# Matmuls without a use in TensorE's waits, weights loaded in the first microseconds: cross attention and two-expert feed-forward, 16 batches

## The reference, cut to what matters

```
x = x + gamma * attention(layernorm(x), ctx, ctx)      # 16 batches of 128 x 256, 8 heads of 16 rows
                                                      # softmax over 256, along the free axis of x
n = layernorm(x)
expert = argmax(softmax(n @ Wg.T))                    # 2 experts
out0 = gelu(n @ W0a.T + b0a) @ W0b.T + b0b            # 256 -> 512 -> 256
out1 = relu(n @ W1a.T + b1a) @ W1b.T + b1b
x = x + (out0 where expert == 0, else out1)
```

## Time and profile before

| | |
|---|---|
| time, median of 3 runs | 248.19 us (248.04 to 249.8) |
| the profiled execution: its own time | 248.95 us |
| its span, first to last instruction | 247.1 us |
| busy: PE, DVE, ACT, POOL | 219.7, 178.1, 144.6, 96.3 us |
| chain that ended last: PE, DVE, ACT, issue | 72%, 12%, 9%, 5% |
| mean granted clock of PE | 0.979 |

### The profile page before, as it was taken

One profiled execution on the slowest core, in us unless ns is written; L12 is line 12 of the kernel. 1 busy time (PEld: TensorE's weight loads), 2 busy tenths in 40 slices (PEclk: granted clock), 3 DMA queues, 4 the chain that ended last, 5 costly groups with the idle time before them and its releaser, 6 DMA issues.

```text
span 247.1 us, 5173 instructions
## 1 busy us (share of the span) xinstructions
PE 219.7 (89%) x2001; PEld 171.3 (69%) x2001; DVE 178.1 (72%) x368; ACT 144.6 (59%) x217; POOL 96.3 (39%) x128
## 2 busy tenths in 40 slices
PE   0477988777898999999999999999999989979995
PEld 0344544444577888788878887888788877959995
DVE  7667476999875988698869886987597715445573
ACT  2012454856667758775877587758774786644140
POOL 8440231333984822482248224823361054032000
PEclk9999999886799999999999999999999999999999
DMA  4227777723330525161516250514111000000101
GB/s 170 100 71 246 247 298 224 273 90 129 88 131 36 183 66 175 10 233 64 176 25 216 65 175 21 178 49 150 20 49 53 16 24 3 21 21 3 41 5 42
DMA packets 18954, 25.86 MB, mean 105 GB/s; under 512 B 1946, under 2 KB 12530, under 8 KB 18674
## 3 DMA queue, kind: packets, MB, share of 16 engines
q1 hardware_dynamic: 17782, 22.63, 27.8%
q10 hardware_dynamic: 1148, 2.90, 3.3%
HBM read 11.28 MB, written 2.10 MB: 54 GB/s over the span
## 4 chain that ended last, share of the span: by engine, by line
PE 72%; DVE 12%; ACT 9%; issue 5%; POOL 0%; DVEq 0%; ACTq 0%; POOLq 0%
PE ff L822 18%; PE ff L852 11%; PE od L765 8%; PE st L753 8%; PE ff L863 6%; PE smax L741 5%; DVE nmax L396 4%; ACT P L600 4%; PE st L728 3%; PE od L773 3%; ACT hid L637 2%; PE od L780 2%; PE smax L714 2%; PE tr L795 1%; DVE qkst L184 1%
## 5 line engine op out<-in xcount | busy, mean ns | idle before, releaser
L600 ACT ACTIVATE P<-st 128x1024 f32<-128x1024 f32 x64 | 65.6, 1025 | 54.1 <-PE st L753 45.6
L396 DVE TENSOR_REDUCE nmax<-smax 128x4 f32<-128x1024 f32 x54 | 66.1, 1224 | 28.8 <-PE smax L741 28.2
L262 POOL TENSOR_TENSOR mv<-mv,power 128x1 f32<-128x1 f32 x31 | 18.3, 591 | 69.2 <-DVE mv L361 69.2
L280 POOL TENSOR_TENSOR hidL<-hid,hidH 128x1024 fp32r<-128x1024 f32 x13 | 31.0, 2387 | 20.6 <-DVE hidH L456 16.2
L822 PE MATMUL ff<-xnTh,w1h 128*128 128x256 f32 x128 | 37.5, 293 | 1.0 <-DVE y L494 1.0
L753 PE MATMUL st<-qkst 64*128 64x256 f32 x240 | 31.1, 338 | 6.6 <-ACT P L600 6.5
L637 ACT ACTIVATE hid<-ff,b1t 128x256 f32<-128x256 f32 x64 | 26.7, 470 | 17.4 <-PE ff L822 17.3
L822 PE MATMUL ff<-xnTh,w1l 128*128 128x256 f32 x128 | 36.0, 281 | 0.0
L822 PE MATMUL ff<-xnTl,w1h 128*128 128x256 f32 x128 | 35.9, 281 | 0.0
L765 PE MATMUL od<-P,vt 128*32 128x256 f32 x512 | 35.7, 426 | 0.1
L852 PE MATMUL ff<-w2h,hidH 128*128 128x256 f32 x124 | 34.2, 309 | 0.0
(11 more groups left out here) (100 smaller groups left out, 344.8 us busy)
## 6 DMA issues: line engine op xcount, KB each, us to landing
qkst<-parts SPq DMA_DIRECT2D x45, 256.0 KB
xv<-in_xv SPq DMA_DIRECT2D x16, 256.0 KB, 2.8
qk<-in_qk SPq DMA_DIRECT2D x15, 256.0 KB, 3.6
out<-y SPq DMA_DIRECT2D x16, 128.0 KB, 2.5
w1t<-in_w ACTq DMA_DIRECT2D x1, 1024.0 KB, 5.4
w2t<-in_w ACTq DMA_DIRECT2D x1, 1024.0 KB, 4.7
qk<-in_first SPq DMA_DIRECT2D x1, 256.0 KB, 3.8
qk<-in_first ACTq DMA_DIRECT2D x1, 256.0 KB, 3.9
```

What stands on the lines that cost most here:

```text
L262: pool.tensor_tensor(mv[:, b % 2, 11:12], mv[:, b % 2, 10:11], power[:, 0:1], ALU.pow).then_inc(s_rstd, 1)
L280: pool.tensor_tensor(hidL[:, units, :], hid[:, units, :], hidH[:, units, :], ALU.subtract).then_inc(s_hidL, 1)
L396: dve.tensor_reduce(nmax[:, c % 2, :, :, j].rearrange("p a e -> p e a"), (ff if c in WIDE and j % 2 else smax)[:, :, :, :], AX.X, ALU.max, ...
L600: act.activation(P[:, b % 2, j, :, :, :].rearrange("p e a l -> p (e a l)"), st[:, :, :, :].rearrange("p e a l -> p (e a l)"), ACT.Exp, sca ...
```

## The change

- **Matmuls without a use.** A new helper `spin` issues matmuls of `onesb` (ones) with `hid` (zeros there, read as 512 bf16 columns) into `od` or `tr`, whose contents nobody needs at that time: 14 before the first real matmul, and 3 to 7 in the slots of the table `SPIN`, 65 in all, the last in slot 15. Each stands in PE's list behind the slot's `maxima`.
- **Weights.** ACT issues `w1t`'s load behind its first two rows instead of in slot 2, and `w2t`'s behind the first `high` instead of in slot 6; the four small loads move from slot 0 to slot -2. The splits move from batches 2 and 3 to batches 1 and 2 on ACT, and from batch 3 to batch 2 on POOL. `gate_and_bias` moves from slots 6 to 12 to slots 0 to 6.
- **Batch 2** is prepared in slot -4, behind the last `take_max0`, instead of in slot -7.
- **One of the four places of `qkst`** is filled by ACT (two ACTIVATEs) instead of DVE (two MEMSETs). DVE sets `onesb` and `hid` first.

```diff
-EARLY = {2: -7, 3: -2}
+EARLY = {2: -4, 3: -2}
+SPIN_FIRST = 14
+SPIN = {-6: 3, -5: 3, -4: 5, -2: 7, -1: 4, 0: 4, 1: 4, 2: 4, 3: 4, 4: 3, 6: 3, 7: 3, 8: 3, 10: 3, 11: 3, 12: 3, 14: 3, 15: 3}
...
+            def spin(bank, count):
+
+                for _ in range(count):
+                    pe.matmul(bank, onesb[:, :], hid[:, 0, :].bitcast(BF16), start=True, stop=True)
...
+                if n <= PAIRS:
+
+                    spin(od[:, :], SPIN.get(n, 0))
+                elif j == 0 and b < 4:
+                    pe.wait_ge(s_mrow, b)
+                    spin_transposes(b)
...
-            fill(dve, 1)
+            dve.memset(onesb[:, :], 1.0).then_inc(s_ones, 1)
+            dve.memset(hid[:, 0, :], 0.0).then_inc(s_ones, 1)
...
-                if 6 <= n < 13:
-                    gate_and_bias(n - 6)
+                if 0 <= n < 7:
+                    gate_and_bias(n)
...
+            act.wait_ge(s_const, 1)
+            for side in range(2):
+
+                act.activation(qkst[:, 1, :, side, :], power[:, 0:1].unsqueeze(2).to_broadcast([128, PAIRS, L]), ACT.Copy,
+                               scale=-2.0 * side).then_inc(s_fill[1], 1)
+            act.dma_start(w1t[:, :, :, :].rearrange("p a e f -> p (a e f)"), w1).then_inc(s_w1, 16)
...
+            act.dma_start(w2t[:, :, :].rearrange("p u l -> p (u l)"), w2).then_inc(s_w2, 16)
```

More of the change, by code:

```diff
@@ L339, in _ @@
                     masks(b - 2)
-                if b == 3 and j >= 2:
+                if b == 2 and j >= 2:
                     pool.wait_ge(s_w2h, j - 1)
@@ L343, in _ @@
                     pool.tensor_tensor(w2l[:, half, :], w2t[:, half, :], w2h[:, half, :], ALU.subtract).then_inc(s_w2l, 1)
-                if b == 3 and j < LC:
+                if b == 2 and j < LC:
                     pool.wait_ge(s_w1h, j + 1)
@@ L662, in _ @@
                     copy_max0()
[L663 to L672, removed]
+                if b == 1 and j < LC:
                     act.wait_ge(s_w1, 16)
                     act.activation(w1h[:, j, :, :], w1t[:, j, :, :], ACT.Copy).then_inc(s_w1h, 1)
-                if b == 3 and j < 2:
+                if b == 2 and j < 2:
                     act.wait_ge(s_w2, 16)
@@ L680, in _ @@
                     high(p)
+                if n == -2:
+                    act.dma_start(wgb[:, :, :].rearrange("p a c -> p (a c)"), wg.partition_broadcast(128)).then_inc(s_small, 16)
+                    act.dma_start(gam[:, :], gamma.partition_broadcast(128)).then_inc(s_small, 16)
+                    act.dma_start(bias_f[:, :], b2.partition_broadcast(128)).then_inc(s_small, 16)
+                    act.dma_start(b1t[:, :], b1).then_inc(s_small, 16)
                 if k == 0 and 2 <= c <= B:
@@ L704, in _, with spin_transposes @@
         def _(pe):
+            def spin(bank, count):
+                for _ in range(count):
+                    pe.matmul(bank, onesb[:, :], hid[:, 0, :].bitcast(BF16), start=True, stop=True)
+            def spin_transposes(b):
+                if b >= 3:
+                    pe.wait_ge(s_xTl, b - 2)
+                spin(tr[:, :, :, :], SPIN.get(n, 0))
             def maxima0(j):
@@ L830, in begin @@
                     pe.wait_ge(s_w2, 16)
-                    pe.wait_ge(s_bias, 7)
-                    pe.wait_ge(s_ones, 2)
+                    pe.wait_ge(s_bias, 8)
                 pe.wait_ge(s_hid, UNITS * (b // 2) + (UNITS if t else UNITS - 2))
@@ L868, in low_pass @@
                     mm.then_inc(s_lastg, 1)
+            pe.wait_ge(s_ones, 2)
+            spin(od[:, :], SPIN_FIRST)
             for n in range(-LEAD, SLOTS):
@@ L909, in _ @@
                         low_pass(b - 4, 0)
+                    if 1 <= b < 4:
+                        pe.wait_ge(s_mrow, b + 1)
+                        spin_transposes(b)
                     if b >= 2:
@@ L912, in _ @@
                 if j == 3 and b >= 1:
+                    if b < 4:
+                        pe.wait_ge(s_ods, b)
+                        spin(od[:, :], SPIN.get(n, 0))
                     transpose_od(b - 1)
```

6 lines of the change are left out of this document (2 added, 4 removed).

## The result

| | before | predicted | changed kernel |
|---|---|---|---|
| median, us | 248.56 (same chip, beside it) | 243.3 (240.9 to 246.6) | 252.97 (251.04, 252.2, 253.74, 254.81) |
| ratio to before | | 0.979 | 1.013, 95% interval 1.008 to 1.019 |
| profiled execution: own time / span | 248.95 / 247.1 | 244.05 | 254.81 / 253.0 |
| first layer's first matmul | 68.42 | 63.5 | 74.35 |
| from there to the end of the span | 178.7 | 178.7 | 178.65 |

The prediction was wrong in sign.

A forecast was written before the change was run, and what follows sets the result against it. PE bounds from 76 us on; before that, PE at the low clock with DVE close behind. 2.8 - 1.4 + 0.2 + 2.0 = 3.6, + 1.4, less 0.1: 4.9 us off 248.95, 244.05; median 243.3 (240.9 to 246.6).

The forecast's parts named there:

- w1t costs nothing: it is issued at 4.8 and moves in 6 to 9.5 us: At the start: w1's early load is free, as it moves while the DMA engines stood still before.
- PE would now be about nine tenths busy: Slots -1 to 2: argument that PE, two thirds busy when its clock fell before, would now stay at the high clock.
- rival C: Clock stays low, decided in slots -1 to 2: added matmuls cost 0.43 us each, +10 to +12, 259 us; chance 0.07.
- 2.1 us of its issue time: ACT ahead of the first exponential: the four small loads take 25.19 to 27.28 in the trace before; exponential predicted at 20.4.
- the first layer starts 37.9 us after that reduction: Slots 1 to 16: from batch 2's first reduction to the first layer 37.9 us instead of 39.3.
- the 1.4 us that were to arrive of PE's 5: Slots 1 to 16: three faster `values` save PE 5 us, of which only 1.4 reach the first layer; DVE 89% busy.
- The stall of 0.8 us behind POOL's splits: Batch 2: `rstd` of batch 1 comes at 57.9 behind the splits, where DVE wants it at 57.1.
- the splits ran beside DVE before too: POOL's splits moved into batch 2: rows of DVE lengthened beside them, but the sum the same with or without the move.
- The reductions without `moments1` between them: Start: batch 2's `moments1` leaves batch 0's reductions; these start at 9.0 to 12.75, the last 2.8 us earlier.
- the slot of 2.4 us: First four slots: 3.1 us for the first, then 2.4 each, instead of 3.2 before.
- my later bound: Batch 1's stacks, loaded beside w2: landing at 15.8 us if w2 goes ahead, 14.8 at even shares; 16.0 taken for `maxima(1)`.
- Rival D: Slot 0: late small loads hold up `gate_and_bias(0)` and DVE's list, each us late one lost; at 28, 246.3; chance 0.10.

The follow-up runs named there:

- e5: e1 with the four small loads and gate_and_bias also back in slots 0 and 6 to 12; 249.3 us, ratio 1.002.
- e12: e9 with w2's load also moved to slot 3, behind the small loads; 244.4 us, ratio 0.978.
- e1: Changed kernel with w1's load issued behind ACT's first K conversion, which waits for batch 1's q and k; 250.27 us, ratio 0.996.
- e4: Kernel before with w1's load alone moved up, right behind ACT's first load; 250.22 us, ratio 1.004.
- e6: Changed kernel with the four small loads and gate_and_bias back in slots 0 and 6 to 12; 253.19 us, ratio 1.019.
- e11: Changed kernel with POOL's four splits alone back in batch 3; 253.45 us.
- e3: Kernel before with only the added matmuls, their waits and the two fills that they read; 250.61 us, ratio 1.002.
- e8: e5 with POOL's four splits back in batch 3; 246.96 us, ratio 0.990.
- e9: e8 with the small loads issued in slot 3 instead of slot 0; 245.43 us, ratio 0.985.
- e7: Kernel before with a list of useless matmuls of three forms ahead of PE's first real one, to test the clock; 290.0 us, compared with nothing.
- e10: e9 without any of the added matmuls; 248.71 us, ratio 0.997.

## Why the prediction was wrong, step by step

Where its steps start, in us of the trace (e5 has w1 and the small loads mended, e12 the whole mended version):

| | predicted | changed | e5 | e12 |
|---|---|---|---|---|
| first `maxima0` | 7.8 | 9.73 | 7.92 | 7.98 |
| last reduction of batch 0 | 12.75 | 18.75 | 13.46 | 13.52 |
| `transpose_max` | 14.1 | 20.74 | 15.45 | 14.89 |
| `maxima(1)` | 16.0 | 21.30 | 17.24 | 15.20 |
| first exponential | 20.4 | 27.27 | 20.70 | 18.76 |
| first reduction of batch 2 | 25.5 | 34.65 | 26.06 | 24.12 |
| slot 4's scores (before: 32.80) | | 43.61 | 32.78 | 30.83 |
| first layer | 63.5 | 74.35 | 69.18 | 64.33 |

**"w1t costs nothing: it is issued at 4.8 and moves in 6 to 9.5 us" is the step that failed first.** I took an ACT-issued DMA to stand in line behind the ACTIVATEs ahead of it. The trace has it at 1.54 us, ahead of them. A wait ahead of it in the list does hold it (in e1 it is issued at 5.64, when q and k are there, and not after the conversion of 0.42 us), but the nearest wait here was for a fill that starts at 0.72 us. So 1 MB ran beside batch 1's q and k; 2.6 us later data (8.22 against 5.64 in e1) and 1.7 us later first maxima (9.73 against 8.07). e1 shows the effect in the changed kernel (2.7 us), e4 the same load's price alone (1.3 us).

**That the added groups hold the clock, for "PE would now be about nine tenths busy", failed next**, and is rival C for slots -6 to 3. Two things were wrong in it. The 14 first matmuls end at 6.67, as predicted ahead of 7.7, but then PE stands for 3.07 us, and the first real matmul runs at clock 0.57. In the three kernels with this hole (the changed one, e6, e11; gaps of 2.7 to 3.4 us) the clock fell in the hole or within 0.2 us of its end; in e1, e3, e5, e8, e9 and e12, where the gap was 0.9 to 2.0 us, it was high there and the rows of the first `maxima0` took 0.48 us or less, not 0.64 to 0.80. And once low it stayed so until about 22.8 us, though PE was busy for all of it, since this stretch is mostly `maxima0`'s form, with 3 to 5 added ones between; e7 shows that this form alone does not hold the clock. It fell in that stretch without the hole too, only later: in e3 and e8 at about 11 us, in e1, e5 and e9 at about 13; in e12 alone it did not. e3 is the plainest case: no hole, and still low for 10 us. With the clock low each added matmul is on the path: at 0.43 us, as rival C had priced it (3 + 3 + 5 of them stand ahead of `transpose_max`). Of the 6.0 us from 12.75 to 18.75, 1.9 are the late data. From the first `maxima0` to the last reduction it is 9.0 us, against 5.5 in e5, so 3.5 go with the low clock, and 0.6 my walk had missed anyway. That the hole brings the clock down at once rests on the comparison of these nine traces; no run changed the hole alone.

**The small loads: "2.1 us of its issue time"** were 3.5 us (23.73 to 27.22), of which one took 2.16, in the same microseconds in which SP issued the three copies of the stacks for 3.47 us. In e1 it was another of the four, 2.28 us, again beside such copies (3.23 us); in e5, issued at 23.18, each took 0.33 to 0.48 us. Why one issue waits is open; I saw it only beside SP's, and not each time: `b1t` in e5, at 24.53 beside copies issued from 24.44 on, took 0.45. Its price in the changed kernel is the exponential at 27.27, 3.06 us behind the start of the scores instead of 2.0, a new hole of PE of 1.59 us, and another fall of the clock, from about 30 until about 43, which e1 shows too behind its hole of 2.43 us and e5 and e6, without one, don't (in e5 it falls at about 33, behind the wait for `mlow`). That is the way from 6.9 us behind the forecast at the exponential to 9.2 at the first reduction of batch 2, and to slot 4 at 43.61. By the rows, moving the small loads back is worth 6.7 us at slot 4 in the changed kernel (e6) and 8.0 in e1 (e5), both single executions. The times show 1.0 us in e5 and nothing in e6, since `gate_and_bias` moved back with them: its copies met the split, and its work came to lie where DVE is the bound. The first of these e8 shows; the second is argued, from DVE's 30.05 us of work behind slot 4 in e9 against 27.9 in the changed kernel. No run moved the loads alone.

**Slots 1 to 16: "the first layer starts 37.9 us after that reduction"** failed last: the 1.4 us that were to arrive of PE's 5 did not. `values` did get fast (1.93 us three times, 4.7 us less in all). But from the first reduction of batch 2 to the first layer it took 39.7 us in the changed kernel, 43.1 in e5 and 40.2 in e12 (39.3 before). In the changed kernel the loss lies ahead of slot 4: 9.0 us to there, at the low clock, where it was 3.7 before; from slot 4 on it took 30.7 us against 35.6. Some of that is DVE's: four of the seven steps of `gate_and_bias` were done by then, and DVE is busy 27.9 us there and not 31.1. In the mended kernels it is the other way round: DVE is the bound, as predicted, at 90% in e9 (33.3 us from slot 4), and PE's gain ends in waits of its own, of which the one for `mlow` at slot 4 is 1.7 us in e5 and in e12. The stall of 0.8 us behind POOL's splits was 0.23 (DVE for the `rstd` ahead of `x_norm` at 69.22). The splits do hold the rows of DVE that they stand beside. The timeline of the changed kernel:

```profile
58.29 0.98 DVE L438 TENSOR_SCALAR xn<-x,mv 128x256 f32<-128x256 f32 x1
...
59.63 2.35 POOL L349 TENSOR_TENSOR w1l<-w1t,w1h 128x1024 fp32r<-128x1024 f32 x1
...
60.79 1.35 DVE L388 TENSOR_SCALAR qk<-qk,mv 128x256 f32<-128x256 f32 x1
```

`q_norm` takes 1.35 us there and 0.40 elsewhere. The forecast had seen this for `x_norm` and put it at no change, as "the splits ran beside DVE before too". For the changed kernel that was nearly right: before, the pair took 0.99 and 0.73 a batch later, and e11 shows no gain from moving the splits. It fails where they meet other rows: in e5 the same splits made 3.27 us of three copies that take 0.91, and e8 against e5, the splits moved alone, is 2.3 us. The Trainium skill's SBUF — State Buffer (SBUF: two separate sides) names the cause, a pair of ports that DVE and POOL lock from each other; the rows agree, and a move of such work changes which rows it meets.

**What was right.** The reductions without `moments1` between them, the slot of 2.4 us (2.46 in e5), `values` at the high clock, and 178.7 us for the rest. `values` was fast all three times only in the changed kernel, e1 and e11, though: e5, e8, e9 and e12 each have one or two slow ones (2.37 to 3.41 us). w2 beside batch 1's stacks was right in kind: 1.15 us of waiting in e5, where the forecast had 1.4, but `maxima(1)` 1.2 us later (16.0 taken, itself 0.2 beyond my later bound; 17.24 in e5; 15.20 without w2). With the first load out of the way e5 was 0.3 us from the forecast at the first exponential and 0.6 at batch 2's first reduction. Some of that is luck: the 1.2 us of `maxima(1)` were made up by the 0.9 that the forecast had given to the small loads ahead of the exponential, which e5 does not have there. Rival D was half right: a transfer did take PE's place (in e5 and e12), not `gate_and_bias`'s inputs, but those of slot 4's scores. Rival C, at 0.07 and 259 us, had the mechanism and its sign; it was to be decided by the clock in slots -1 to 2, and in the changed kernel it was high for only the first two of these. It should have had far more weight, since the trace of before shows no matmul of 16 or 17 rows at the high clock. The mended version's 4.1 us are all won in the start: its first reduction of batch 2 is 5.0 us earlier than before, its first layer 4.1.

## What to carry to other kernels

A load that is moved to the front competes with the first operands from the moment at which its engine can issue it, and here that was not behind the arithmetic written ahead of it: hold it back by a wait on the data that must come first. Here fillers for the clock paid only where the holes they can't fill were short (e9 against e10), and with work between them that lets the clock fall they brought nothing even so (e3); ahead of a late operand the clock was lost again and they cost their full length, so the data comes first and the fillers after it. A split or copy on POOL is to be placed by which rows of DVE it stands beside, not only by POOL's free time. And an edit that moves a load together with the work on it can hide what the load costs: look at the rows between, not only at the time (e6).

## What the runs showed of the hardware that I had not expected

- DMAs in ACT's list are issued past its unfinished work: at 1.54 us with a table load (until 2.72) and two ACTIVATEs (until 4.74) ahead of it in the list.
- 40 fp32 matmuls of 16 rows, gap-free for 11.87 us, let the granted clock fall from 1.00 to 0.50, and 128 fp32r ones of 63 rows don't (e7). Matmuls of zeros do lift it: the 14 first ones of the changed kernel took 5.35 us, where 14 at 0.43 are 6.0.
- The same kernel gets different clocks in different executions, and its time follows: e11 from 247.4 us at 0.972 to 255.0 at 0.946, e1 246.2 at 0.979 to 252.2 at 0.951. Not all of the spread is the clock's: thirteen of the kernel before, beside e12, took 247.96 to 250.53 at 0.979 or 0.986.
- One small DMA in four took 2.16 us (changed kernel) and 2.28 us (e1) of its engine's time to issue, beside another engine's three issues; in e5 each took 0.33 to 0.48, one of them beside such issues too.
- A small transfer can be late on its own: `mlow`, 8 KB from SBUF to SBUF, took 4.47 us from issue to landing in e5 and 3.28 in e9; in e5 the DMA engines moved 358 GB/s between 28 and 33 us.
